# Routing an expert layer's tokens in three groups during the layer before it, with a fixed region of memory for each expert

## What is computed

```
xn = layernorm(x)
s = windowed attention(xn)                    # 16 heads, causal window of 64
g = silu(xn @ ternary(W).T * alpha + bias)
x = x + s * g                                 # first layer
xn = layernorm(x)
s = Chebyshev linear attention(xn)            # running sums over the tokens
logits = xn @ router_w.T + router_b           # 8 experts, the best 2 are taken
for e in range(8):                            # 128 -> 512 -> 128 with gelu
    cw = the softmax weight of expert e, 0 where it was not chosen
    out += expert_e(xn) * cw
g = silu(layernorm(out + xn) * ln_w + ln_b)
x = x + s * g                                 # second layer
```

## Time and profile before

| | |
|---|---|
| median of 3 runs | 885.68 us (882.62 to 885.87) |
| profiled execution, its own time | 883.1 us |
| its span | 881.3 us |
| busy: PE / DVE / ACT / POOL | 583.4 / 652.7 / 444.7 / 434.3 us |
| mean granted TensorE clock | 0.871 |

### The profile page before, as it was taken

How to read it: one execution, slowest core, us unless ns; L and a number is a source line. 1 busy time by engine, 2 the same in 40 slices (tenths; PEclk the granted TensorE clock), 3 DMA queues, 4 the chain that set the end, 5 groups by cost and what they waited for, 6 DMA issues and landing times.

```text
span 881.3 us, 21985 instructions
## 1 busy us (share of the span) xinstructions
PE 583.4 (66%) x7047; PEld 394.8 (45%) x7047; DVE 652.7 (74%) x1667; ACT 444.7 (50%) x1075; POOL 434.3 (49%) x697
## 2 busy tenths in 40 slices
PE   1888788878788878853544277777777777732120
PEld 0465555555555555542222145555555555421110
DVE  4588777777777777755878078989898989737766
ACT  1365555545555555521343277878787878400001
POOL 3134444544444555442777444444444444277873
PEclk9999999999999999985575599999999999955555
DMA  9920000000000000000111303333333332112221
GB/s 236 344 59 3 3 3 0 0 0 0 0 0 0 0 0 0 2 1 12 52 49 66 99 25 97 97 97 97 97 97 97 97 97 97 36 48 66 57 66 51
DMA packets 64527, 49.53 MB, mean 56 GB/s; under 512 B 10057, under 2 KB 55377, under 8 KB 64465
## 3 DMA queue, kind: packets, MB, share of 16 engines
q1 hardware_dynamic: 59328, 39.74, 14.4%
q0 software_dynamic: 5136, 9.02, 3.8%
HBM read 18.83 MB, written 18.35 MB: 42 GB/s over the span
## 4 chain that ended last, share of the span: by engine, by line
PE 32%; DVE 24%; POOL 17%; issue 17%; ACT 5%; DMA 2%; DVEq 2%; SPq 0%; POOLq 0%; ACTq 0%
POOL experts_sb L541 7%; POOL xbuf L528 7%; PE m_ps L988 4%; PE p_ps L869 4%; PE e_ps L1000 4%; DVE yts L1306 3%; PE q_ps L899 2%; PE y_ps L951 2%; ACT vd L603 2%; PE p_ps L944 2%; DVE x_all L1151 2%; DVE pr L1303 2%; DVE rot L1120 2%; ACT xs L608 1%; PE y_ps L832 1%
## 5 line engine op out<-in xcount | busy, mean ns | idle before, releaser
L576 ACT ACTIVATE pexp<-e_ps 128x512 f32<-128x512 f32 x128 | 76.4, 597 | 76.3 <-PE e_ps L816 74.7
L988 PE MATMUL m_ps<-xs,wb 128*128 128x512 f16 x276 | 80.6, 404 | 19.7 <-issue 18.4
L1087 DVE TENSOR_REDUCE mneg<-m_ps 128x4 bf16<-128x512 f32 x128 | 84.5, 681 | 5.1 <-PE m_ps L783 5.0
L541 POOL DMA_INDIRECT experts_sb<-ybuf,slots x64 | 66.1, 1033 | 28.7 <-issue 18.5
L528 POOL DMA_INDIRECT xbuf<-x,slots x64 | 63.3, 990 | 33.9 <-issue 19.2
L492 POOL COPY xs<-xs 128x128 f16<-128x128 f16 x32 | 12.8, 400 | 107.3 <-ACT xs L608 107.3
L603 ACT COPY vd<-p_ps 64x64 f32<-64x64 f32 x128 | 27.0, 211 | 73.1 <-DVE early L1122 70.8
L1046 PE MATMUL e_ps<-b_sb,cwt 8*128 8x128 f32 x64 | 16.6, 436 | 63.7 <-ACT cwt L744 63.7
L832 PE MATMUL y_ps<-pexp,vd 128*32 128x128 f32 x512 | 55.1, 284 | 2.7 <-ACT pexp L576 0.6
L1262 DVE TENSOR_SCALAR early<-p_ps 128x256 f32<-128x256 f32 x32 | 13.6, 424 | 55.3 <-ACT vs L650 55.3
L960 PE MATMUL p_ps<-eye_sb,yn 128*128 128x128 f32 x32 | 11.6, 364 | 63.7 <-DVE yn L1311 63.7
(11 more groups left out here) (218 smaller groups left out, 2125.6 us busy)
## 6 DMA issues: line engine op xcount, KB each, us to landing
wb<-experts_sb SPq DMA_DIRECT2D x46, 256.0 KB, 2.4
xbuf<-zero_sb SPq DMA_DIRECT2D x23, 256.0 KB, 4.3
xs<-xbuf SPq DMA_DIRECT2D x23, 256.0 KB, 3.0
ybuf<-rt SPq DMA_DIRECT2D x23, 256.0 KB, 2.5
experts_sb<-in_experts_w SPq DMA_DIRECT2D x8, 512.0 KB, 6.5
x_all<-in_x SPq DMA_DIRECT2D x8, 256.0 KB, 5.5
xbuf<-x,slots POOLq DMA_INDIRECT x64, 2.2
experts_sb<-ybuf,slots POOLq DMA_INDIRECT x64, 2.6
```

Of the source, the lines that this page charges most:

```text
L541: nc.gpsimd.indirect_dma_start(yg[:, 2 * (B * n + b) + k, :], None, ybuf, bass.IndirectOffsetOnAxis(ap=slots[:, k, B * n + b:B * n + b + 1 ...
L576: nc.scalar.activation(pexp[:, j, :, :], e_ps[j % 2][:, :, :], ACT.Exp, scale=float(D) ** -0.5).then_inc(exp_ready.sem, 1)
L988: last = nc.tensor.matmul(u_ps[f % 2], wb1[:, i % 2, f, a, :], xg16[:, i % 2, b, :], start=k == 0, stop=k == len(PARTS) - 1)
L1087: nc.vector.tensor_reduce(mneg[:, n.batch, j // 2, (j % 2) * NG:(j % 2) * NG + NG], m_ps[j % 2][:, :, :], AX.X, ALU.max, negate=True).then ...
```

## The change

- The tiles are routed in three groups: 0 to 13, 14 to 27, 28 to 31. For each, DVE runs `choose(g)` (13 operations), PE `count(g)` (15, 15 and 5 matmuls), DVE `place(g)` (7 operations). `choose(0)` stands behind head 19, `count(0)` and `place(0)` behind head 23, `choose(1)` behind head 33, `count(1)` and `place(1)` behind head 34, group 2 at the end. `owners()` (12 operations) follows.
- Each expert has a fixed region of 4096 rows, so a slot is known before the totals are. `xbuf` and `ybuf` have 71 blocks of 512 rows for it, and SP writes zeros over all of both: 142 transfers instead of 23. A pass reads which block it takes from `owner`'s second row: one more `value_load` ahead of each `load_rows` and each `store`.
- POOL sends 3 transfers in each of the steps of heads 24 to 32 and one in head 33 (28 in all), 10 behind head 35, 6 behind head 36 and 20 at the end.
- LEAD is 4: steps 0 to 2 of the second loop have no pass, pass 22 ends in c = 26, and steps 27 to 31 have none.
- At the end POOL gathers groups 0 to 4 at once and group n + 5 behind `deviation(n)`. The expert output is staged in `vd` instead of `rt`.

```diff
-LEAD = 8
+LEAD = 4
+GROUPS = [(0, 14), (14, 28), (28, 32)]
+BLOCKS = PASSES - 1 + E * E - 2 * B * T // SLOT + 1
...
+            for buf, sem_, zeros in ((xbuf, s_zeroed, zero_sb[:, :]), (ybuf, s_y_zeroed, zero_sb[:, :].bitcast(F32))):
+                for i in range(BLOCKS):
...
             def load_rows(i):
                 after(sp, s_rows_transposed, i - 1)
-                sp.dma_start(xin[:, i % 2, :, :], xbuf[SLOT * i:SLOT * i + SLOT, :].rearrange("(k p) c -> p k c", p=P)).then_inc(s_rows_in[i % 2], 16)
+                place = sp.value_load(owner[0:1, 1, i:i + 1], min_val=0, max_val=BLOCKS - 1)
+                sp.dma_start(xin[:, i % 2, :, :], xbuf[bass.ds(place * SLOT, SLOT), :].rearrange("(k p) c -> p k c", p=P)).then_inc(s_rows_in[i % 2], 16)
...
+            def send(rows):
+                for i in range(sent[0], sent[0] + rows):
+                    n, k = i // 2, i % 2
+                    for g in range(3):
+                        if i == 2 * GROUPS[g][0]:
+                            pool.wait_ge(s_slots, g + 1)
+                    pool.wait_ge(xn1_stored.sem, 4 * (n + 1))
+                    nc.gpsimd.indirect_dma_start(xbuf, bass.IndirectOffsetOnAxis(ap=slots[:, k, n:n + 1], axis=0), x16[:, n, :], None).then_inc(s_scattered, 16)
+                sent[0] += rows
...
+            with pool.Fori(2, 6) as t:
+                for k in range(4):
+                    step(Tile(t, k))
+            pool.wait_ge(s_zeroed, 16 * BLOCKS)
+            for n in range(8):
+                step(Tile(6, n), 2, 1)
+            step(Tile(TAUS, 0), 2, 1)
+            step(Tile(TAUS, 1), 0, 1)
+            step(Tile(TAUS, 2))
+            step(Tile(TAUS, 3))
+            send(10)
+            step(Tile(TAUS, 4))
+            send(6)
+            step(Tile(TAUS, 5))
+            send(2 * NT - sent[0])
             for i in range(PASSES):
                 low_parts(i)
             pool.wait_ge(s_rows_out[0], 16 * ((PASSES + 1) // 2))
             pool.wait_ge(s_rows_out[1], 16 * (PASSES // 2))
-            gather(0)
-            gather(1)
+            for n in range(5):
+                gather(n)
             for n in range(TAUS):
                 deviation(n)
-                if n + 2 < TAUS:
-                    gather(n + 2)
+                if n + 5 < TAUS:
+                    gather(n + 5)
...
+            def choose(g):
+                lo, hi = GROUPS[g]
+                n = hi - lo
...
+            def place(g):
+                dve.wait_ge(s_counted, g + 1)
...
+            with dve.Fori(2, 5) as t:
+                for k in range(4):
+                    step(Tile(t, k))
+            choose(0)
+            with dve.Fori(5, 6) as t:
+                for k in range(4):
+                    step(Tile(t, k))
+            place(0)
+            with dve.Fori(6, TAUS) as t:
                 for k in range(4):
                     step(Tile(t, k))
             for n in range(6):
                 step(Tile(TAUS, n))
+                if n == 1:
+                    choose(1)
+                if n == 2:
+                    place(1)
+            choose(2)
+            place(2)
+            owners()
```

212 lines of the change are left out of this document (121 added, 91 removed).

## The result

The changed kernel takes 872.29 us (median of 4 runs, 869.91 to 875.58) where the kernel before takes 884.86 (4 runs beside it): a ratio of 0.9868, 95% interval 0.9845 to 0.9892, so it is 1.3% faster. The kernel was run a second time later, on another chip: 869.26 against 883.20, ratio 0.9839 (0.9816 to 0.9862). The forecast was 874.5. The profiled execution's span goes from 881.3 to 871.2, so by -10.1 where -11.2 was forecast.

The account below looks back on a forecast made before the run. Two stretches were taken as bound by GpSimd's indirect transfers, scatter and gather. Terms 13.1 - 5.8 + 1.5 + 1 - 41.7 + 35.2 - 14.5 = -11.2 gave 874.5 us on the median's scale, 8 in 10 between 863 and 884.

Parts of the forecast that it names:

- Routing at the end, -5.8: From the first layer's end to clip(0): the remaining routing takes 8.65 us instead of 14.45.
- Routing in the first layer, +13.1: Four uncovered routing blocks on VectorE ahead of L1094 lengthen the first layer by 13.1 us, bounds 8 to 17.
- Sends, +1.5: Scatter transfers in GpSimd's first-layer waits mostly fit; nine steps at 0.15 us cost 1.5, bounds 0 and 9.
- Rival 1: First-layer transfers are held up beside VectorE: 15 us in the loop, c = 3 13 late, time 902; chance 0.12.
- the port rule: VectorE and GpSimd share a port pair and GpSimd's descriptors starve: some 37 us lost ahead of L492; not used in the sum.
- Zeros, +1: SP's 142 zero transfers beside the first layer's first rounds may share the transfer engines: 1 us, bounds 0 and 8.
- Lead, -41.7: From clip(0) to the first tile with a pass: 54.3 us instead of 96.0, SP's queue last, scatter landed 2 us ahead.
- Late steps, +35.2: Second loop's end: four more steps without a pass at 8.8 us each add 35.2; passes as many as before.
- End, -14.5: From the start of c = 31 to the end: 96.3 us instead of 110.8, with gathers begun earlier.
- Rival 3: First layer: VectorE's waits shrink while it routes, so routing costs 5 instead of 13.1; time 866, chance 0.15.
- Rival 2: First-layer routing costs 17 + 8 for 14.1, or half the end's 14.5 is lost; time 878.5 to 889.5, chance 0.20.

Follow-up runs that it names:

- e5_clock: Changed kernel with 18 more unused matmuls on TensorE in head 34, ahead of its wait for the scaling behind choose(1); ratio 0.9834 to the kernel before.
- e8_sends_late: Changed kernel with the 28 row transfers of group 0 sent behind the first layer's loop instead of in it; ratio 1.0069, kernel before 910.25 us there.
- e1: Changed kernel with two groups of the end's gathers sent at once instead of five; ratio 0.9897 to the kernel before.
- e2: Changed kernel with four groups of the end's gathers sent at once instead of five; ratio 0.9815 to the kernel before.
- e4: Changed kernel with operations of choose(0), choose(1) and place(1) put into VectorE's waits inside heads, place(0) still a block; ratio 0.9679 to the kernel before.
- e11: Changed kernel with routing operations in VectorE's waits, four groups of gathers at once and weight loads first on SP's queue; 852.65 us, ratio 0.9641.
- e12: Changed kernel with 3 leading tiles instead of 4 (its first deviation and end are at X + 12.7 and X + 91.1); ratio 0.9865 to the kernel before.
- starred runs: The runs of e3, e6_lead8, e7_lead8_gather2 and e8_sends_late, together on a chip where the kernel before takes 910.25 us.
- e3: Changed kernel with weight loads of passes 0 and 1 ahead of the carried rows on SP's queue; ratio 0.9714, kernel before 910.25 us there.
- e6_lead8: Changed kernel with 8 leading tiles instead of 4, five groups of gathers at once; ratio 1.0094, kernel before 910.25 us there.
- e7_lead8_gather2: Changed kernel with 8 leading tiles instead of 4 and two groups of gathers at once instead of five; ratio 0.9755, kernel before 910.25 us there.

## Why the prediction came out, point by point

- **Routing at the end, -5.8:** 413.91 to 421.86 is 7.95 instead of 8.65, so -6.5. As forecast.
- **Routing in the first layer, +13.1: too small, 19.2.** The step that failed is "choose(0) 4.0, place(0) 2.0, choose(1) 4.0, place(1) 2.0" as the whole price. VectorE's operations have those lengths, and it is true that nothing covers them there. Left out was what the wait does to TensorE: it then runs at half clock, and VectorE waits for it in turn. e5_clock takes that away at two places and gives back 3.9, and at `place(0)` the traces in which the clock stayed up have 1.2 to 1.4 less. At `choose(0)` the 1.6 above VectorE's 3.8 were not tested by themselves. Without these three the four places cost 12.2 to 12.5, so that as the price at full clock the forecast was near. 19.2 also lies outside the bounds of 8 to 17. In the second run of the same kernel it was 16.5.
- **Sends, +1.5:** nothing. Steps 20 to 27 are 11.21 on the mean against 11.36, -1.2 in all, but e8_sends_late, which sends nothing there, has 11.21 too, so this is not the transfers' doing; from tile 0 to T their price is 0.5 at most. The 0.2 us of room ahead of L519 is there (0.18 in head 25), and that was enough: the 28 transfers take 0.96 to 1.16 each.
- **Rival 1 and the port rule.** In the first layer the transfers are as fast as in the lead of before, 0.96 and little more. What the Trainium skill says of starving descriptors ("SBUF — State Buffer", Who interferes with whom) does not show in these 28 transfers, and this rival's 15 us in the loop are not there. The 620 and 3100 ns that the prediction quotes stand on that page of the Trainium skill under another heading ("A bandwidth-pool intuition that's wrong"), and are told there of one VectorE instruction, `tensor_copy`.
- **Zeros, +1:** nothing. Tile 0 to tile 15 takes the same in both kernels to 0.01 us.
- **Lead, -41.7:** -42.8. The forecast had SP's queue last and the scatter 2 us ahead of it. In this trace the two end together, and in e1, e2, e4 and e5 SP's queue is last by about 1.3; e11 and e12 show what the scatter alone allows.
- **Late steps, +35.2:** +35.6. The passes keep their pace, and gathers beside the last steps don't lengthen them.
- **End, -14.5:** -12.3. Deviations 0 and 3 are 0.8 and 0.7 late, with 1.30 us for a gather instead of 1.26, and 1.07 from a deviation's start to its gate (828.84 to 829.91) were not in the sum; the other 0.4 are in the gates and combines. The text's "four gates and three combines" leave one gate out: 96.3 comes out with five, from deviation 3 on, and five is what the program's order has.
- **Rival 3**, the ring takes up the routing: not as the change puts it. e4_filled shows that the ring does take it up when the operations stand in VectorE's waits.
- **Rival 2**, routing dearer and a part of the end lost: both came in part (+6.1 where it had 10.9, +2.2 where it had 7.2), and together. Of its mechanism (counts and loop boundaries set back, slower gathers) only 0.5 us more of wait for the counts of `place(1)` and 0.04 us a gather did. The time still is near the forecast because the other terms lie the other way: sends and the steps around them -2.7, lead -1.1, zeros -1, the routing's end -0.7, and 1.8 in the start, which is chance. The sum was right to 1.1 us with one term wrong by 6, and that is luck.

## What to carry to other kernels

A block of small operations on one engine, put ahead of what TensorE waits for, costs its own length and, where the clock then falls, again what TensorE loses at half clock; put into that engine's own waits, operation by operation, it cost nearly nothing here (16 us against 0.3 to 0.8). When transfers are sent ahead on a queue that also carries short work for others, count the work that stands behind them: two, four and five groups at once ended at X + 101.1, X + 93.6 and X + 98.5. Before a limit is called a latency of the hardware, look at the order of the queue behind it: of 23.9 us of "first pass" 8.4 were not there once the weights stood ahead of the small rows.

## What the runs showed of the hardware

- TensorE at 2.4 GHz falls to 1.2 after waits of 4.55 and 4.63 us in otherwise dense work, in every trace that has them. After one of 1.43 to 1.45 us at `place(0)` it falls in ten traces of thirteen and stays up in three, with a step of 14.2 to 14.7 us where it falls and 13.3 to 13.5 where it stays up. How soon it comes back differs too between two executions of one kernel (back by 392 us in one, not by 400 in the other): 2.5 us of spread in the total.
- Rows are asked for 2.97 us behind the start of the last of GpSimd's scatters, where nothing else holds SP (2.97 and 2.98 in e12_lead3 and e11_best; on the chip of the starred runs 3.9 in e3 and 4.9 in e8).
- On one chip (kernel before: 910.25) the four programs that ran there stop in ways that no trace of the other chips shows; none of the four ran on another chip. VectorE in e3_loads_first:

```profile
766.16 0.29 DVE L1394 TENSOR_TENSOR yn<-yts,dn 128x128 f32<-128x128 f32 x1 [0.71 <-DVE dn L1392]
780.97 0.60 DVE L1386 TENSOR_TENSOR pr<-early,y_ps 128x432 f32<-128x432 f32 x1 [14.51 <-remote]
```

Its input was ready by 770.9, so some 10 of these 14.51 us have no cause in the program's own waits. e8_sends_late has 13.11 at the same line, e6_lead8 8.95 at L1445; all three lie beside GpSimd's gathers or right behind them. e7_lead8_gather2, with 16 gathers at once, has none of VectorE, but like e6 one of ScalarE in the lead, 6.51 at L682, beside the scatters. What stops the engines there is open: no run took the transfers away, and the kernel before was not profiled on that chip.
